# A graph network's second attention: two edge-attribute steps to each main step in its first half, the edge projection in its second, edge places by a tree of sums

## The reference

```python
# layer 0, twice (the second time with the residual)
e    = leaky_relu(el[src] + er[dst], 0.2)
ex   = exp(e - segment_max(e, dst)[dst])
rst  = segment_sum(feat[src] * (ex / segment_sum(ex, dst)[dst]), dst)
# layer 1
edge_proj = edge_attr @ W_sum + b_sum            # 50000 x 128 by 128 x 256
sum3d     = segment_sum(edge_proj, src)          # by source node
x + z_in[in_deg] + z_out[out_deg] + cent_term + vor_term + sum3d
```

## Time and profile before

| | |
|---|---|
| median of 3 runs (lowest to highest) | 3311.61 us (3309.6 to 3315.16) |
| the profiled execution | 3313.14 us, its span 3311.4 us |
| TensorE matmul / weight load | 2198.6 us (66%) / 1597.2 us (48%) |
| VectorE | 2090.0 us (63%) |
| ScalarE | 1434.6 us (43%) |
| GpSimd | 2385.0 us (72%) |
| granted TensorE clock, mean | 0.843 |
| second attention's steps | 1166.91 us to 1611.88 us after the span's start |
| middle | 1614.2 us to about 1760 us |

### The profile page before, as it was taken

The page is one execution under the profiler, slowest core; times in us unless marked ns, Lnnn a source line. Parts: engine busy times, 40 slices in busy tenths (PEclk is TensorE's granted clock), DMA queues, the critical chain, the costliest instruction groups (busy, mean ns, idle before and its releaser), DMA issues. The chain is left out here.

```text
span 3311.4 us, 73877 instructions
## 1 busy us (share of the span) xinstructions
PE 2198.6 (66%) x11487; PEld 1597.2 (48%) x11488; DVE 2090.0 (63%) x5467; ACT 1434.6 (43%) x4736; POOL 2385.0 (72%) x2419
## 2 busy tenths in 40 slices
PE   6566377777656367766696666676666677566668
PEld 2365255555455355555443444454444456344446
DVE  8899867775599967776694444464444454444446
ACT  2866399998666389998581000031000014000004
POOL 7877767777777767777655777775777773777773
PEclk9789789998899789998797778697777798777778
DMA  5488744443688745443694333443333332333332
GB/s 166 127 225 227 215 114 141 141 128 104 179 231 227 210 132 161 138 128 104 162 287 154 109 109 109 125 125 108 109 109 109 109 104 79 110 109 109 109 107 80
DMA packets 346745, 466.05 MB, mean 141 GB/s; under 512 B 111880, under 2 KB 262249, under 8 KB 343185
## 3 DMA queue, kind: packets, MB, share of 16 engines
q0 software_dynamic: 111952, 284.59, 29.7%
q1 hardware_dynamic: 161584, 111.23, 11.6%
q10 hardware_dynamic: 72852, 67.08, 7.4%
HBM read 385.50 MB, written 76.97 MB: 140 GB/s over the span
## 5 line engine op out<-in xcount | busy, mean ns | idle before, releaser
L400 PE MATMUL t_ps<-t_ring,shared 128*128 x2640 | 901.4, 494 | 497.2 <-ACTq L237 397.4
L400 PEld LDWEIGHTS t_ps<-t_ring,shared 128*128 128x128 f32 x2640 | 598.3, 243 | 790.5 <-issue 703.2
L186 POOL DMA_INDIRECT ring<-feat_d,srcC x784 | 771.0, 983 | 260.3 <-issue 215.4
L186 POOL DMA_INDIRECT t_ring<-feat_d,srcC x758 | 719.6, 949 | 288.4 <-issue 214.4
L265 ACT ACTIVATE ring<-ring,exC 128x64 f32<-128x64 f32 x3136 | 787.9, 335 | 0.2
L400 PE MATMUL bank<-ring,arena 128*128 x1408 | 434.6, 435 | 161.7 <-ACT ring L265 117.6
L318 DVE TENSOR_TENSOR acc<-acc,t_ps 128x256 f32 x440 | 185.2, 421 | 502.6 <-PE t_ps L400 499.7
L608 POOL DMA_INDIRECT attr_d<-abuf,attr_pos x392 | 403.0, 1028 | 117.7 <-issue 117.7
L186 POOL DMA_INDIRECT t_ring<-rel_d,relC x379 | 359.8, 949 | 160.6 <-issue 106.2
L302 DVE TENSOR_SCALAR shared<-lane,dlocT,weightT 128x128 f32<-128x128 f32 x1320 | 407.7, 362 | 50.9 <-issue 29.2
L1828 ACT COPY t_ring<-t_pt 128x512 f32<-128x512 f32 (+1 forms) x14 | 7.7, 553 | 882.9 <-PE t_pt L1795 882.9
(11 more groups left out here) (297 smaller groups left out, 2731.3 us busy)
## 6 DMA issues: line engine op xcount, KB each, us to landing
arena<-lo_d ACTq DMA_DIRECT2D x392, 128.0 KB
rel_d<-mid_stage SPq DMA_DIRECT2D x25, 1024.0 KB, 4.8
arena<-attr_d SPq DMA_DIRECT2D x98, 260.0 KB, 3.0
abuf<-in_attr SPq DMA_DIRECT2D x56, 448.0 KB
t_ring<-feat_d SPq DMA_DIRECT2D x1536, 1.0 KB
t_ring<-feat_d ACTq DMA_DIRECT2D x1536, 1.0 KB
ring<-feat_d,srcC POOLq DMA_INDIRECT x784
t_ring<-rel_d SPq DMA_DIRECT2D x768, 1.0 KB
```

Of the source, the lines that this page charges most:

```text
L186: pool.indirect_dma_start(out=ring[:, u % RING, j, 0:D], out_offset=None, in_=table, in_offset=bass.IndirectOffsetOnAxis(ap=index[:, u, j: ...
L400: last = pe.matmul(ps[k % len(ps)][:, 0:g.width], hot[:, k % NHOT, j, :], ring[:, slot, j, 0:g.width], start=(j == 0), stop=(j == 1))
```

## The change

In ga1 (ga0 stays as it was) two new functions take the place of add_steps and multiply_steps. Steps 0 to 109 (PAST) now carry two attribute steps each, 2s and 2s + 1, so all 220 attribute steps are done in the first half; steps 110 to 219 carry none. The main sums are added three steps behind (SOON) and not four, the attribute sums a step behind. Attribute products go to four banks of their own (`pa`), main ones to four banks. Attribute numbers are loaded apart, 22 registers on VectorE and 20 on TensorE for each ten steps. Turns 1 to 4 are the loop on VectorE (turns 0 to 4 on TensorE), the others are written out.

From step 112 on, every fourth step turns and projects one tile of attribute sums (pe_attr_rows, dve_attr_rows); VectorE makes the copy, the bias term and the sum into `term`. W_sum and b_sum are loaded by SyncE early in ga1. The same work is gone from the middle. The places of the edges are summed over the 25 tiles by a tree of adds and not by one reduction.

```diff
@@ constants
-AHEAD = 14
+PAST = T // 2
+DEEP = 4
+SOON = LAG - 1
@@ new, beside add_steps and multiply_steps
+def add_steps_ahead(dve, tag, g, hot, ps, acc, hot_a, aring, pa, between, extra):
+    regs = [dve.alloc_register(f"{tag}_tiles{k}") for k in range(TURN + 1)]
+    aregs = [dve.alloc_register(f"{tag}_attr_tiles{k}") for k in range(TURN + 2)]
+    main_tile, attr_tile, attr_slot = (dve.alloc_register(f"{tag}_{x}")
+                                       for x in ("tile", "attr_tile", "attr_slot"))
+    row = 32 * (2 + g.attr)
+    def make_hot(s, k):
+        dve.wait_ge(g.step_done, s + 1)
+        dve.tensor_tensor(
+            hot[:, k % NHOT, :, :], lane[:, :].unsqueeze(1).to_broadcast([P, 2, P]),
+            dlocT[:, bass.ds(s, 1), :].rearrange("p s j -> p (s j)").unsqueeze(2)
+            .to_broadcast([P, 2, P]), ALU.is_equal).then_inc(g.hot_made, 1)
+    def make_attr_hot(a, k, q):
+        dve.reg_alu(attr_slot, aregs[q], 10, ALU.logical_shift_right)
+        slot = dve.snap(attr_slot, min_val=0, max_val=ARING - 1)
+        dve.wait_ge(g.attr_done, a + 1 + NHOT - DEEP)
+        dve.wait_ge(g.attr_ready, a + 1)
+        dve.tensor_scalar(hot_a[:, k % DEEP, :], lane[:, :], aring[:, slot, AW - 1:AW],
+                          minus_tile[:, g.attr, bass.ds(a, 1)], ALU.subtract, ALU.is_equal)\
+           .then_inc(g.attr_hot_made, 1)
+    def add_step(s, k, q):
+        dve.reg_alu(main_tile, regs[q], 31, ALU.bitwise_and)
+        tile = dve.snap(main_tile, min_val=0, max_val=NT - 1)
+        dve.wait_ge(g.step_done, s + (NHOT + 1))
+        dve.wait_ge(g.added, s + NHOT)
+        dve.tensor_tensor(acc[:, tile, 0:g.width], acc[:, tile, 0:g.width],
+                          ps[k % len(ps)][:, 0:g.width], ALU.add).then_inc(g.added, 1)
+    def add_attr(a, k, q):
+        dve.reg_alu(attr_tile, aregs[q], 5, ALU.logical_shift_right)
+        dve.reg_alu(attr_tile, attr_tile, 31, ALU.bitwise_and)
+        tile = dve.snap(attr_tile, min_val=0, max_val=NT - 1)
+        dve.wait_ge(g.attr_done, a + (NHOT + 1))
+        dve.wait_ge(g.attr_added, a + NHOT)
+        dve.tensor_tensor(acc_a[:, tile, :], acc_a[:, tile, :], pa[k % DEEP][:, 0:AW - 1],
+                          ALU.add).then_inc(g.attr_added, 1)
+    def turn(i):
+        known = isinstance(i, int)
+        dve.reg_load(regs, tiles[row:row + 1, bass.ds(TURN * i, TURN + 1)])
+        for k in range(TURN):
+            s = TURN * i + k
+            ahead = not known or s < PAST
+            if ahead and k % (TURN // 2) == 0:
+                dve.reg_load(aregs, tiles[row:row + 1, bass.ds(2 * TURN * i + 2 * k, TURN + 2)])
+            if known and s == PAST:
+                dve.reg_load(aregs[0:2], tiles[row:row + 1, T + 2:T + 4])
+            if known and s == SOON:
+                between()
+            if known and s == 0:
+                for j in range(2):
+                    make_attr_hot(j, j, j)
+            make_hot(s, k)
+            for j in range(2 if not known or 1 <= s <= PAST else 0):
+                add_attr(2 * TURN * i + 2 * k - 2 + j, 2 * k + 2 * TURN - 2 + j,
+                         j if known and s == PAST else 2 * k % TURN + 2 + j)
+            for j in range(2 if not known or s + 1 < PAST else 0):
+                make_attr_hot(2 * TURN * i + 2 * k + 2 + j, 2 * k + 2 + j, 2 * k % TURN + 2 + j)
+            if not known or s >= SOON:
+                add_step(s - SOON, k + TURN - SOON, k + LAG - SOON)
+            if known and s > PAST:
+                extra(s)
+    turn(0)
+    with dve.Fori(1, PAST // TURN) as i:
+        turn(i)
+    for i in range(PAST // TURN, T // TURN):
+        turn(i)
+    dve.reg_load(regs[0:SOON], tiles[row:row + 1, T + LAG - SOON:T + LAG])
+    for k in range(SOON):
+        add_step(T - SOON + k, T - SOON + k, k)
+def multiply_steps_ahead(pe, tag, g, ring, hot, ps, hot_a, aring, pa, extra):
+    regs = [pe.alloc_register(f"{tag}_slots{k}") for k in range(TURN)]
+    aregs = [pe.alloc_register(f"{tag}_attr_slots{k}") for k in range(TURN)]
+    main_slot, attr_slot, pairs, need = (pe.alloc_register(f"{tag}_{x}")
+                                         for x in ("slot", "attr_slot", "pairs", "need"))
+    row = 32 * g.attr
+    pe.sem_inc(g.step_done, NHOT)
+    pe.sem_inc(g.added, NHOT)
+    pe.sem_inc(g.attr_done, NHOT)
+    pe.sem_inc(g.attr_added, NHOT)
+    def turn(i):
+        known = isinstance(i, int)
+        pe.reg_load(regs, slots[row:row + 1, bass.ds(TURN * i, TURN)])
+        for k in range(TURN):
+            s = TURN * i + k
+            ahead = not known or s < PAST
+            if ahead and k % (TURN // 2) == 0:
+                pe.reg_load(aregs, slots[row:row + 1, bass.ds(2 * TURN * i + 2 * k, TURN)])
+            for j in range(2 if ahead else 0):
+                a, q = 2 * TURN * i + 2 * k + j, 2 * k + j
+                pe.reg_alu(attr_slot, aregs[q % TURN], 5, ALU.logical_shift_right)
+                pe.reg_alu(attr_slot, attr_slot, ARING - 1, ALU.bitwise_and)
+                slot = pe.snap(attr_slot, min_val=0, max_val=ARING - 1)
+                pe.wait_ge(g.attr_hot_made, a + 1)
+                pe.wait_ge(g.attr_added, a + 1 + NHOT - DEEP)
+                pe.matmul(pa[q % DEEP][:, 0:AW - 1], hot_a[:, q % DEEP, :],
+                          aring[:, slot, 0:AW - 1], start=True, stop=True).then_inc(g.attr_done, 1)
+            pe.reg_alu(main_slot, regs[k], 31, ALU.bitwise_and)
+            slot = pe.snap(main_slot, min_val=0, max_val=RING - 1)
+            pe.reg_alu(pairs, regs[k], 11, ALU.logical_shift_right)
+            pe.reg_alu(need, pairs, 1, ALU.max)
+            pe.wait_ge(g.hot_made, s + 1)
+            pe.wait_ge(g.added, s + 1 + NHOT - len(ps))
+            pe.wait_ge(g.pair_ready, need)
+            for j in range(2):
+                last = pe.matmul(ps[k % len(ps)][:, 0:g.width], hot[:, k % NHOT, j, :],
+                                 ring[:, slot, j, 0:g.width], start=(j == 0), stop=(j == 1))
+            last.then_inc(g.step_done, 1)
+            if known and s > PAST:
+                extra(s)
+    with pe.Fori(0, PAST // TURN) as i:
+        turn(i)
+    for i in range(PAST // TURN, T // TURN):
+        turn(i)
@@ buffers of the attention phase
+pa = [wide[b][:, j, :] for b in range(2) for j in range(2)]
+wsum, bsum = aa[1][:, 0, :], aa[1][:, 1, :]
+at_rows = wx[1][:, :, :].rearrange("p c m -> p (c m)")[:, 0:4 * P].rearrange("p (k m) -> p k m", k=4)
@@ load_terms (SyncE, between the loads of the second attention)
+if k == 5:
+    sp.wait_ge(s_wx, 2)
+    sp.dma_start(wsum, t["L1_gnn_W_sum"]).then_inc(s_w, 16)
+    sp.dma_start(bsum, t["L1_gnn_b_sum"].unsqueeze(0).to_broadcast([P, D])).then_inc(s_w, 16)
@@ place_columns
-dve.reduce_sum(pos[:, r], running[:, :, r].rearrange("p n j -> p j n"), AX.X)
-dve.drain()
+sum_tiles(dve, r)
+def sum_tiles(dve, r):
+    n = NT - 1
+    while n % 2 == 0:
+        n //= 2
+        dve.tensor_tensor(running[:, 0:n, r], running[:, 0:n, r], running[:, n:2 * n, r], ALU.add)
+        dve.drain()
+    dve.tensor_tensor(pos[:, r], running[:, 0, r], running[:, NT - 1, r], ALU.add)
+    dve.drain()
+    for k in range(1, n):
+        dve.tensor_tensor(pos[:, r], pos[:, r], running[:, k, r], ALU.add)
+        dve.drain()
@@ new, before the block
+SUM_FROM = PAST + 2
+def pe_attr_rows(pe, s):
+    n, rest = divmod(s - SUM_FROM, 4)
+    if n < 0 or rest:
+        return
+    if 1 <= n <= NT:
+        if n == 1:
+            pe.wait_ge(s_w, 16 * 8)
+        pe.wait_ge(s_turned, 2 * NT + n)
+        pe.matmul(pa[(n - 1) % 4][:, P:P + D], at_rows[:, (n - 1) % 4, :], wsum,
+                  start=True, stop=True).then_inc(s_proj, 1)
+    if n < NT:
+        if n == 0:
+            pe.wait_ge(steps[1].attr_added, T + NHOT)
+        if n >= 4:
+            pe.wait_ge(s_feat, 2 * NT + n - 3)
+        pe.transpose(pa[n % 4][:, 0:P], acc_a[:, n, 0:P], ident[:, :]).then_inc(s_turn, 1)
+def dve_attr_rows(dve, s):
+    n, rest = divmod(s - SUM_FROM - 3, 4)
+    if 0 <= n < NT and not rest:
+        dve.wait_ge(s_turn, 2 * NT + n + 1)
+        if n >= 4:
+            dve.wait_ge(s_proj, 2 * NT + n - 3)
+        dve.tensor_copy(at_rows[:, n % 4, :], pa[n % 4][:, 0:P]).then_inc(s_turned, 1)
+    n, rest = divmod(s - SUM_FROM - 6, 4)
+    if 0 <= n < NT and not rest:
+        if n == 0:
+            dve.wait_ge(steps[1].attr_added, T + NHOT)
+            dve.wait_ge(s_w, 16 * 8)
+            for k in range(5):
+                dve.wait_ge(s_back[k], TERM_STORES[k] + 16)
+        dve.scalar_tensor_tensor(out=term[:, n, :], in0=bsum, scalar=acc_a[:, n, AD:AD + 1], in1=term[:, n, :],
+                                 op0=ALU.mult, op1=ALU.add).then_inc(s_row, 1)
+    n, rest = divmod(s - SUM_FROM - 7, 4)
+    if 0 <= n < NT and not rest:
+        dve.wait_ge(s_row, 2 * NT + n + 1)
+        dve.wait_ge(s_proj, 2 * NT + n + 1)
+        dve.tensor_tensor(term[:, n, :], term[:, n, :], pa[n % 4][:, P:P + D], ALU.add).then_inc(s_feat, 1)
@@ the block
```

(24 more changed lines are left out.)

48 lines of the change are left out of this document (2 added, 46 removed).

## The result

The changed kernel takes **3380.69 us** (median of 4 runs, 3378.63 to 3383.58), the kernel before 3311.65 us beside it: 1.0205 times the time before, 95% interval 1.0193 to 1.0217. That is 69 us more. I had predicted 3349 us, 37 us more, and a range up to 3372 us. The direction was right, the size was not, and the time lies outside the range.

The account below looks back on a forecast made before the run. The prediction took GpSimd's gathers to bound ga1, ScalarE close behind, and VectorE to set its first half after the change. ga1 +50, middle -13 and places 0 sum to +37 us: 3349 us against 3311.6, range 3318 to 3372.

Parts of the forecast that it names:

- who is last, and why the loss stays: ga1: VectorE sets the first half; ScalarE, only three pairs ahead, cannot recover; GpSimd no longer last; ga1 +50 us.
- the first half: ga1 to step 110: steps, register loads, jumps, zeroing and short stands on VectorE together take 293 us.
- I take 2.40 ... Written out ... I take 1.95: VectorE's first-half steps in ga1: 2.40 us each in the loop (192 us), 1.95 us each written out (58.5 us).
- the head of ga1: VectorE's turn heads: two register loads, 3.1 us, five times after the first; jumps 3.03 us each.
- the middle: Between ga1 and tail: removed VectorE work, 12.2 us from iteration 4 on, gives -13 us, bounds -16 and -4.
- come when they come: Middle before iteration 4: VectorE waits for z_out's rows; an iteration's three bias terms save at most 2 us there.
- Rival 2: The middle is bound by DMA, so only 4 us come back: 3358 us, chance 0.14.
- the places: Tree sum over 25 tiles: VectorE saves 6 us, but behind it waits for ScalarE's masks: 0, bounds -5 and +1.
- The rule weighed: First-half register loads: about 200 ns per register, not 68, would add 49 us: 3398 us, chance 0.01.
- Rival 1: VectorE's queue work is hidden: first half 224 us, GpSimd stays last in ga1, 3299 us, chance 0.12.
- Its turning point: The change is not slower if ga1's first half takes under 256 us, a loop step under 1.94 us.
- Rival 3: TensorE at half clock through ga1's first half costs 38 us, through half of it 19: 3368 us, chance 0.10.

Follow-up runs that it names:

- e3: Changed kernel with the attribute sums apart and VectorE's loop written out: 3318.11 us, ratio 1.0020 to the kernel before.
- e7: Changed kernel with ScalarE allowed 12 pairs ahead of TensorE in ga1, not 3: 3367.27 us, ratio 1.0169 to the kernel before.
- e1: Changed kernel with the two attribute sums of a first-half step no longer following each other: 3363.75 us, ratio 1.0150 to the kernel before.
- e5: Kernel before with the changed kernel's middle, the projected sum of edge attributes left out altogether: 3295.88 us, ratio 0.9946 to the kernel before.
- e4: Kernel before with only the tree of sums for the places: 3316.49 us against 3314.04, ratio 1.0010.
- e11: e10 with every attribute register load begun at a multiple of four words and made of whole fours: 3296.16 us against the kernel before's 3314.48.
- e12: e11 with the places summed by the one reduction of the kernel before, not the tree: 3291.49 us, ratio 0.9927 to the kernel before.
- e10: e3 with three attribute steps to two main ones over steps 0 to 146, projection every second step: 3319.51 us, ratio 1.0020 to the kernel before.
- e2: Changed kernel with VectorE's loop over turns 1 to 4 written out: 3345.05 us, ratio 1.0098 to the kernel before.

## Why the prediction was right and wrong

**Right: who is last, and why the loss stays.** VectorE sets the first half, ScalarE the second, GpSimd neither, and ScalarE's three pairs of lead make the loss final (e3, e7). The second half was forecast at 199.5 + 2.3 = 201.8 us and is 202.2.

**Wrong: the first half.** Forecast 293 us, measured 316.7, and 3.1 us more in front of it. The step that failed is "I take 2.40 ... Written out ... I take 1.95". Measured are 2.52 us in the loop, over my upper bound of 2.50, and 2.30 written out. 80 x 0.12 and 30 x 0.35 are 9.6 and 10.5 us. I had priced each added instruction by its pitch between other instructions, where nothing of its own kind was near, and had not read that `add_attr` waits for the sum before it. The order of rows that I showed has the two sums next to each other; the wait was in the code beside them. e1 takes the price apart: without the stand the loop step is 2.38 us, near my 2.40, and the written-out step 2.02, near my 1.95.

**Wrong: the head of ga1.** I counted the two loads "at a head ... five times after the first" and took the first as it was. But there too a second load (22 registers, 1.82 us) and two attribute one-hots (0.73 us) now stand in front of the first main one-hot: 3.1 us in all. A jump cost 3.4 and not 3.0 us; I had taken it against a head of 1.53 us that the row puts down to TensorE and not to the load.

**Wrong size: the middle.** Forecast -13, measured -17.6 (-18 in e5). From iteration 4 on I had 12.2 us and the trace shows 12.4. The rest is the start. The failed step is that z_out's rows "come when they come": VectorE could go on with them 2.9 us earlier after ga1's end (18.1 us and not 21.0), since GpSimd's wait for the first z_in to land fell from 3.80 to 0.89 us; and behind that wait VectorE's own instructions took 2.3 us less. That the loads of W_sum and the bias no longer ran beside the z_in gathers is a possible cause of the first, but no run tells it. Rival 2, the DMA bound, is wrong: with a share of 1.01 before, all of VectorE's time still came back.

**Wrong sign, small: the places.** I had 0 with bounds -5 and +1; the two comparisons (e4, and e11 against e12) show 2 and 6 us lost, neither far from noise. I looked for who waits on VectorE there and not for who shares a resource with it. VectorE's own gain was 3.0 us (18.0 less 15.0), not 6.

**The rule weighed.** My rows gave 68 ns a register, the Trainium skill (Runtime: NRT & Kernel Launch, Instruction fetch mechanics) about 200 ns, and I gave the rule 0.01. For this change that was right in result: 21 registers take 1.61 us and 22 take 1.82. But e10 shows the other price, 4.06 us for 18, 226 ns each, where the load does not begin at a multiple of four words. The Trainium skill's figure is near this one; it does not hold for the aligned loads of these kernels.

**The rivals.** Rival 1 (the queue's work hidden) is refuted by e2: writing out the loop alone gives 36 us. Its turning point, a first half of 256 us, can be checked: e3 has 258.2 us and stands 0.2% over the time before, with 3 us lost in front of it. Rival 3 (the clock) did not come: the granted clock in the first half is 0.88 to 0.94, so mostly the level of 2.4 GHz (0.88 to 0.97 in the first half before), and the attribute sums wait 3.2 us in all for TensorE, against 21.7 us for one another. The sum of the corrected terms, 9.6 + 10.5 + 3.1 + about 1 for the jumps, takes +50 to +74; ga1 grew by 77, so 3 us stay open.

## What to carry to other kernels

Work moved onto an engine with room on average is to be priced in the place where it lands, with the queue's rows and the waits of its own kind in the new order: two accumulations into one buffer should have another instruction between them. Where one engine may run only a few items ahead of the next, slack lost early does not come back, so spread the added work thinly enough (here three to two in place of four to two) that it never becomes the bound. Begin register loads at multiples of four words, and look at what an edit does to the start of every load that shares the table. When an engine's own gain is hidden, ask what its new instructions do to the engine beside it.
